# Expert results added onto the residual rows by indirect DMA, in place of a closing gather stage

## The reference, cut to what matters

```python
def _L1_ffn_ref(x, Wg, bg, W1, b1, W2, b2):
    gate_scores = x @ Wg + bg
    _, idx = jax.lax.top_k(gate_scores, K)                     # K = 2 of E = 8
    mask = jax.nn.one_hot(idx, E, dtype=x.dtype).sum(axis=-2)
    h = jax.nn.gelu(jnp.einsum('td,edh->teh', xf, W1) + b1[None], approximate=False)
    y = jnp.einsum('teh,ehd->ted', h, W2) + b2[None]
    out = jnp.einsum('ted,te->td', y, mf)
...
x = x + _L1_ffn_ref(_layernorm(x, axis=-1)[None], ...)[0]      # the residual is added last
```

## Time and profile before

| | us |
|---|---|
| median of 3 runs | 7423.68 (7422.31 to 7426.34) |
| the profiled execution | 7418.85 |
| its span, first to last instruction | 7417.1 |
| routing, about | 5878 to 6365 |
| filling, about | 6373 to 6390 |
| experts, about | 6390 to 7157 |
| closing, about | 7159 to 7417 |

### The profile page before, as it was taken

One profiled execution on the slowest core, in us unless ns is written; L12 is line 12 of the kernel. 1 busy time (PEld: TensorE's weight loads), 2 busy tenths in 40 slices (PEclk: granted clock), 3 DMA queues, 4 the chain that ended last, 5 costly groups with the idle time before them and its releaser, 6 DMA issues. The chain is left out here.

```text
span 7417.1 us, 130762 instructions
## 1 busy us (share of the span) xinstructions
PE 5086.8 (69%) x27158; PEld 4303.4 (58%) x27158; DVE 4225.4 (57%) x12806; ACT 2168.8 (29%) x5921; POOL 4011.9 (54%) x4739
## 2 busy tenths in 40 slices
PE   9955555555555699965267776777777666699950
PEld 3445555555555699963156555665665544699950
DVE  5565555555555433345567777777777677433333
ACT  3300000000000133322134444444444444466640
POOL 1157777777777400002377777777777377300027
PEclk9977777777777799988667777667767655799985
DMA  8843333333333211106544444444444333222246
GB/s 275 301 152 105 105 105 105 105 104 104 105 105 105 86 52 53 53 31 195 176 114 115 113 114 113 115 113 114 113 115 113 113 112 111 80 70 71 70 121 198
DMA packets 520513, 856.27 MB, mean 115 GB/s; under 512 B 99091, under 2 KB 378979, under 8 KB 519430
## 3 DMA queue, kind: packets, MB, share of 16 engines
q0 software_dynamic: 179568, 497.45, 24.1%
q1 hardware_dynamic: 210614, 228.31, 9.9%
q10 hardware_dynamic: 130144, 128.87, 5.0%
HBM read 615.20 MB, written 239.07 MB: 115 GB/s over the span
## 5 line engine op out<-in xcount | busy, mean ns | idle before, releaser
L1069 POOL DMA_INDIRECT s_rows<-xp_table,s_index x1664 | 1638.3, 985 | 506.9 <-issue 452.4
L323 POOL DMA_INDIRECT s_rows<-rel_table,s_staged x1664 | 1579.7, 949 | 535.3 <-issue 491.0
L352 PE MATMUL s_part<-s_pick,s_rows 128*128 128x128 f32 x6656 | 1196.5, 353 | 920.0 <-DMA s_rows<-rel_table,s_staged 688.8
L352 PEld LDWEIGHTS s_part<-s_pick,s_rows 128*128 128x128 f32 x6656 | 1106.9, 259 | 1010.0 <-DVE s_pick L360 959.0
L1190 PE MATMUL s_part<-s_pick,s_scaled 128*128 128x128 f32 x6656 | 1430.4, 374 | 371.3 <-DVE s_scaled L1346 354.0
L1190 PEld LDWEIGHTS s_part<-s_pick,s_scaled 128*128 128x128 f32 x6656 | 1206.5, 266 | 564.6 <-issue 289.0
L373 DVE TENSOR_TENSOR sums<-sums,s_part 128x256 f32 x1666 | 701.8, 421 | 931.5 <-PE s_part L352 747.6
L1361 DVE SCALAR_TENSOR_TENSOR sums<-sums,s_old_share,s_part 128x256 f32 x1666 | 793.1, 476 | 403.4 <-PE s_part L1190 253.3
L1103 ACT ACTIVATE s_apart<-window,s_local 128x128 f32<-128x128 f32 x1664 | 531.7, 390 | 1153.9 <-PE s_part L1190 1101.4
L1346 DVE TENSOR_TENSOR s_scaled<-s_rows,s_share 128x256 f32<-128x256 f32 x1664 | 687.1, 413 | 84.1 <-issue 83.0
L2126 POOL DMA_INDIRECT s_got<-y_rows,s_staged x196 | 189.0, 964 | 832.9 <-ACT s_staged L2100 774.5
(11 more groups left out here) (306 smaller groups left out, 6450.2 us busy)
## 6 DMA issues: line engine op xcount, KB each, us to landing
rel_table<-s_rows ACTq DMA_DIRECT2D x98, 1024.0 KB
s_rows<-rel_table,s_staged POOLq DMA_INDIRECT x1664, 2.7
s_rows<-xp_table,s_index POOLq DMA_INDIRECT x1664
s_rows<-exp_rows SPq DMA_DIRECT2D x204, 128.0 KB, 2.0
y_rows<-s_y SPq DMA_DIRECT2D x204, 128.0 KB, 1.7
s_x<-in_x SPq DMA_DIRECT2D x196, 128.0 KB, 2.2
s_mid<-mid_rows SPq DMA_DIRECT2D x98, 256.0 KB
x_rows<-s_x SPq DMA_DIRECT2D x196, 128.0 KB, 1.7
```

Source lines behind the costliest of these rows:

```text
L323: pool.indirect_dma_start(out=rows[:, s, :], out_offset=None, in_=rel_table[:, :], in_offset=bass.IndirectOffsetOnAxis(ap=staged[:, 2 * s ...
L352: mm = pe.matmul(part[s % PARTS][:, k, :], rows[:, s, k * P:(k + 1) * P], pick[:, s % PICKS, :], start=True, stop=True)
L1069: pool.indirect_dma_start(out=rows[:, b * BATCH + s, :], out_offset=None, in_=xp_table[:, :], in_offset=bass.IndirectOffsetOnAxis(ap=index ...
```

## The change

`x3_rows` becomes `sums_out`, which the routing stage fills with the residual rows as before. The rows of `exp_rows` grow from 256 to EXT = 264 floats, and ACT writes each row's token number into element 256 (one more ACT operation per tile); the filling rows carry numbers from NP on, which name spare rows behind the tokens. In the expert stage POOL turns the token numbers of each loaded tile into integers (`keep_ids`), waits for `y` and for the DMA of the tile before, and issues one indirect DMA that adds `y` onto `sums_out` (`add_to_out`). SP no longer stores `y`, and its next load waits for `keep_ids` too. DVE's buffer of `y` is free again when the adding DMA of two tiles before has landed. When all 204 have landed, SP and ACT each copy one half of `sums_out` to `out` by a plain DMA. The closing stage, `y_rows`, `place_all`, `mask_all` and the six operations that used them go.

```diff
-    x3_rows = dram("x3_rows", [NP, D])
-    exp_rows = dram("exp_rows", [X * CAP + X * P, D])
-    y_rows = dram("y_rows", [TILES * P, D])
+    sums_out = dram("sums_out", [NP + P, D])
+    exp_rows = dram("exp_rows", [X * CAP + X * P, EXT])
...
-                        pool.wait_ge(moved_done, 2 * t + 2)
+                        pool.wait_ge(moved_done, 3 * t + 3)
                         pool.sem_inc(scatter_go, 1)
...
+                    pool.iota(token_i[:, :], pattern=[[P, NT]], base=0, channel_multiplier=1).then_inc(const_i, 1)
+                    pool.wait_ge(const, 4)
...
-                        act.activation(moved[:, b, :].rearrange("p (k c) -> p k c", k=HALVES), sums[:, :, ds(t * P, P)], ACT.Copy).then_inc(moved_done, 1)
+                        act.activation(moved[:, b, 0:D].rearrange("p (k c) -> p k c", k=HALVES), sums[:, :, ds(t * P, P)], ACT.Copy).then_inc(moved_done, 1)
+                        act.activation(moved[:, b, D:D + 1], token[:, ds(t, 1)], ACT.Copy).then_inc(moved_done, 1)
...
-                        v.tensor_scalar(mask_all[:, ds(t, 1), :].rearrange("p o x -> p (o x)"), rank[:, b, :], 2.0, None, ALU.is_lt)
...
-                        v.tensor_copy(place_all[:, ds(t, 1), :].rearrange("p o x -> p (o x)"), place[:, b, :]).then_inc(place_step, 1)
...
+                    v.tensor_scalar(zeros[:, D:D + 1], line[:, :], float(NP), None, ALU.add).then_inc(zero_made, 1)
...
-                    then(v.tensor_tensor(place_all[:, :, :], place_all[:, :, :], shift[:, :].unsqueeze(1).broadcast_to([P, NT, X]), ALU.add))
-                    then(v.tensor_tensor(place_all[:, :, :], place_all[:, :, :], mask_all[:, :, :], ALU.mult))
-                    then(v.tensor_reduce(both[:, :], place_all[:, :, :], AX.X, ALU.add))
-                    then(v.tensor_reduce(second[:, :], place_all[:, :, :], AX.X, ALU.max))
-                    then(v.tensor_tensor(slots[:, :, 0], both[:, :], second[:, :], ALU.subtract))
-                    then(v.tensor_copy(slots[:, :, 1], second[:, :]))
...
+            def copy_out(eng, k):
+
+                eng.wait_ge(y_out, 16 * TILES)
+                half = slice(k * (NP // 2), (k + 1) * (NP // 2))
+                eng.dma_start(out[half, :].rearrange("(q r) d -> q (r d)", r=16),
+                              sums_out[half, :].rearrange("(q r) d -> q (r d)", r=16)).then_inc(copied, 16)
+                eng.wait_ge(copied, 32)
...
-                    def store(t, b):
-                        sp.wait_ge(y_done, t + 1)
-                        sp.dma_start(y_rows[ds(t * P, P), :], y[:, b, :]).then_inc(y_out[b], 16)
-
                     def step(t, i, b, left):
                         if left == 2:
                             sp.wait_ge(turned, t + 1)
+                            sp.wait_ge(ids_kept, t + 1)
                             load(t + 2, b)
-                        if not isinstance(t, int) or t > 0:
-                            store(t - 1, 1 - b)
 
                     load(0, 0)
                     load(1, 1)
                     by_tiles(sp, step, TILES // 2)
-                    store(TILES - 1, (TILES - 1) % 2)
-                    for b in range(2):
-                        sp.wait_ge(y_out[b], 16 * (TILES // 2))
+                    copy_out(sp, 0)
+
+                @block.gpsimd
+                def _(pool):
+                    def keep_ids(t, i, b, s):
+                        pool.wait_ge(rows_in[b], 16 * i + 16)
+                        pool.sem_inc(ids_go, 1)
+                        pool.tensor_copy(ids[:, s, :], rows[:, b, D:D + 1]).then_inc(ids_kept, 1)
+
+                    def add_to_out(t, b, s):
+
+                        pool.wait_ge(y_done, t + 1)
+                        wait_past(pool, y_out, 16 * t)
+                        pool.wait_ge(ids_kept, t + 1)
+                        pool.sem_inc(out_go, 1)
+                        pool.indirect_dma_start(out=sums_out[:, :], in_=y[:, b, :], in_offset=None,
+                                                out_offset=bass.IndirectOffsetOnAxis(ap=ids[:, s, :], axis=0),
+                                                compute_op=ALU.add).then_inc(y_out, 16)
+
+                    for t in range(2):
+                        keep_ids(t, 0, t, t)
+                    for t in range(2):
+                        keep_ids(t + 2, 1, t, t + 2)
+                        add_to_out(t, t, t)
+                    with pool.Fori(0, TILES // 4 - 1) as i:
+                        for j in range(4):
+                            keep_ids(4 * i + j + 4, 2 * i + 2 + j // 2, j % 2, j)
+                            add_to_out(4 * i + j + 2, j % 2, (j + 2) % 4)
+                    for t in range(TILES - 2, TILES):
+                        add_to_out(t, t % 2, t % 4)
+                    pool.wait_ge(y_out, 16 * TILES)
...
-                        wait_past(v, y_out[b], 16 * i)
+                        wait_past(v, y_out, 16 * t - 16)
                         v.tensor_tensor(y[:, b, :], psY[b], b2_now[:, b, :], ALU.add).then_inc(y_done, 1)
...
-        with ExitStack() as st:
-            x3 = at(st, "s12_x3", [P, RING, D])
...
```

More of the change, by code:

```diff
@@ L50 @@
 TILES = 2 * NT + X
-RING = 7
+IDS = 4
 EXT = D + 2 * HEADS
@@ L1517, in gnn_kernel @@
             staged = at(st, "s9_staged", [P, 2, 2], I32)
-            moved = at(st, "s9_moved", [P, 2, D])
+            moved = at(st, "s9_moved", [P, 2, EXT])
+            token_i = at(st, "s9_token_i", [P, NT], I32)
+            token = at(st, "s9_token", [P, NT])
             psX = [bank(st, f"s9_psX{b}", D) for b in range(2)]
@@ L1542, in step @@
                         sp.wait_ge(x3_done, t + 1)
-                        sp.dma_start(x3_rows[ds(t * P, P), :], x3[:, b, :]).then_inc(x3_out[b], 16)
+                        sp.dma_start(sums_out[ds(t * P, P), :], x3[:, b, :]).then_inc(x3_out[b], 16)
                     load(0, 0)
@@ L1635, in move @@
                         act.activation(staged[:, b, :], slots[:, ds(t, 1), :].rearrange("p o j -> p (o j)"), ACT.Copy).then_inc(moved_done, 1)
-                        act.activation(moved[:, b, :].rearrange("p (k c) -> p k c", k=HALVES), sums[:, :, ds(t * P, P)], ACT.Copy).then_inc(moved_done, 1)
+                        act.activation(moved[:, b, 0:D].rearrange("p (k c) -> p k c", k=HALVES), sums[:, :, ds(t * P, P)], ACT.Copy).then_inc(moved_done, 1)
+                        act.activation(moved[:, b, D:D + 1], token[:, ds(t, 1)], ACT.Copy).then_inc(moved_done, 1)
                     hold(0, 0)
                     hold(1, 1)
+                    act.wait_ge(const, 4)
+                    for b in range(2):
+                        act.activation(moved[:, b, D + 1:EXT], window[:, 0:EXT - D - 1], ACT.Copy)
                     exp_below(0, 0)
@@ L1811, in last_places @@
                         note(t, b)
-                    v.wait_ge(const_i, 3)
+                    v.wait_ge(const_i, 4)
+                    v.tensor_copy(token[:, :], token_i[:, :]).then_inc(const, 1)
                     v.tensor_scalar(lower[:, :, :], lower_i[:, :, :], 0.5, None, ALU.is_gt).then_inc(const, 1)
@@ L1845, in gnn_kernel @@
             shift = at(st, "s10_shift", [P, X])
-            both = at(st, "s10_both", [P, NT])
-            second = at(st, "s10_second", [P, NT])
             over = at(st, "s10_over", [1, TILES, X])
@@ L1904, in _ @@
                     then(v.tensor_scalar(tile_exp[:, :], exp_f[:, :], float(X - 1), None, ALU.min))
[L1906 to L1911 removed]
         scores_of.close()
         with ExitStack() as st:
[L1917 removed]
+            rows = at(st, "s11_rows", [P, 2, EXT])
+            ids = at(st, "s11_ids", [P, IDS, 1], I32)
             hT = at(st, "s11_hT", [P, 2, HALVES, P])
@@ L1926, in gnn_kernel @@
             psY = [bank(st, f"s11_psY{b}", D) for b in range(2)]
-            rows_in, y_out = [sem(f"s11_rows_in{b}") for b in range(2)], [sem(f"s11_y_out{b}") for b in range(2)]
+            rows_in, y_out = [sem(f"s11_rows_in{b}") for b in range(2)], sem("s11_y_out")
+            ids_go, ids_kept, out_go = sem("s11_ids_go"), sem("s11_ids_kept"), sem("s11_out_go")
+            copied = sem("s11_copied")
             w1_go, w1_ready, w2_go, w2_ready, b2_ready = (sem(f"s11_{n}") for n in ("w1_go", "w1_ready", "w2_go", "w2_ready", "b2_ready"))
             turned, hT_ready, up_done, active, down_done, y_done = (sem(f"s11_{n}") for n in ("turned", "hT_ready", "up_done", "active", "down_done", "y_done"))
+            def copy_out(eng, k):
[4 more added lines that the diff above has]
+                eng.wait_ge(copied, 32)
             def expert(eng, t):
@@ L1992, in _ @@
                     by_tiles(act, step, TILES // 2)
+                    copy_out(act, 1)
                 @block.tensor
```

92 lines of the change are left out of this document (12 added, 80 removed).

## The result

| | before | after |
|---|---|---|
| median of 20 runs each, us | 7423.52 (7418.7 to 7429.5) | 7439.92 (7434.34 to 7448.0) |
| the profiled execution | 7418.85 | 7448.0 |
| its span | 7417.1 | 7446.3 |
| first y of the expert stage starts | 6401.2 | 6414.7 |
| last y starts | 7157.0 | 7395.0 |

The ratio after to before is 1.0022, with a 95% interval of 1.0015 to 1.0028: the change makes the kernel slower by 16 us, 0.2%. 7231 was forecast, in a range of 7180 to 7400; the result lies outside both. Rival (3), the chain of adding DMAs that takes over the expert stage, had named 7455.

The account below looks back on a forecast made before the run. TensorE was taken to bound the expert stage, POOL the routing and closing stages. Last y's end 7157.4 + 5.1 + 66 + 1.9, less 5 and 0.5, gave a span of 7225, a median of 7231 us; range 7180 to 7400.

Parts of the forecast that it names:

- Rival (3): Expert stage: the chain of adding DMAs takes over and eats the whole gain; 4.8 us a tile, 7455 us, slower; chance 0.12.
- The adding DMAs: Expert stage: landing taken as 3.0 us, between 2.4 and 4.4; chain 3.4 us a tile, hidden by TensorE's 3.72.
- The cover: Expert stage: the room in which TensorE's 3.72 us a tile hides the chain, up to a landing of 3.3 us.
- The reissue: Expert stage: 0.40 us from POOL's instruction before to the adding DMA's issue, added to the landing for each tile.
- The tail: End of the expert stage: the last adding DMA lands 5.1 us after the last y.
- The copy: After the last add: plain copy from memory to memory, 66 us with issue and landing; bounds 32 and 125.
- Routing: Routing stage, bounded by POOL: two DVE operations go, taken as -5 us, ends -20 and +5.
- Filling: Filling stage: DVE's six last operations go and POOL takes DVE's place, -0.5 us.
- The closing stage: After the last y: the stage is removed, and all 259.7 us to the span's end go.
- (1): Expert stage: adding DMA lands after 3.3 to 4.2 us; 7329, or 7370 with a lower TensorE clock; chance 0.22.
- (2): Expert stage: DVE's copies stretch POOL's issue; 7237 with 0.35 us, 7370 with the whole 0.99; chance 0.13.
- (4): Final copy: carried by few DMA engines, it takes 250 us instead of 64; 7417 us; chance 0.03.

## Why the prediction was wrong

**The adding DMAs: here it failed.** "I take 3.0" for the landing; it is 4.0, inside the stated ends of 2.4 and 4.4 and near the upper. The cover ended at 3.3. I had added to a scatter the 0.3 by which a gather is dearer and 0.3 for the second stream at the bulk rate. Neither prices what the runs showed, an add that costs 1.6 us over the plain scatter and grows with the rows (2.9, 3.4 and 4.0 for 32, 64 and 128). The upper end had been built from what the DMA does, a whole read and then a whole write, and would have been the better choice, 0.4 us off where 3.0 was 1.0 off.

**The reissue, in the same sum: failed too.** 0.4 us came from rows in which POOL followed an instruction of its own with no wait. Behind a wait it is 0.83. The two misses add up to 1.00 + 0.43, over a cover of 0.32 (3.72 less the 3.4 of the sum): 1.11 us a tile, 226 us by 204 tiles, against 224.5 measured. At a landing of 4.0 with my 0.4 the chain would have been 4.4 us, +139. With the true restart the cover ended at a landing of 2.89, below my own 3.0.

**The tail** was 8.6 us and not 5.1, by the same two terms. **The copy** was 41.9 us instead of 66, inside the bounds of 32 and 125: 12.85 MB in 41.9 us are 307 GB/s, and each byte is read and written. The Trainium skill (DMA: Bandwidth & Descriptors, Latency and other measured facts) has 207 to 214 GB/s per direction for copies with pieces of 16 KB and a harmless pitch. That is too low for this copy of pieces of 57 KB on two queues; the measurement decides. **Routing** gained nothing where 5 were taken: the scatter's mean fell from 1124 to 1095 ns, and POOL's busy time of the stretch stayed. **Filling** +1.8 instead of -0.5. **The closing stage** went as predicted, all 259.7 us. Two slips of the prediction's own arithmetic changed nothing: with the copy at 125 and routing at +5 its upper end is 7300 and not 7295, and "faster" adds up to 0.85 and a little more, not 0.84.

By terms, from the forecast span of 7225 to 7446.3: +224.5 stage, +3.5 tail, -24 copy, -1.5 end, +5 routing, +2.3 filling, +11.8 ahead of it all, together +221.6, the 221.3 between the spans but for rounding.

**The rivals.** (3) was right in its mechanism and its 4.8 us a tile, partly by luck: 4.4 + 0.4 where 4.0 + 0.83 stand. It had 0.12. (1) was right that the landing is above the cover, but its 3.3 to 4.2 were summed with the short restart, and its loss of the clock did not come: 1.00 at a PE busy for 82%. (2) is real and worth 0.2 us a tile, and only once the chain is on the path. (4) fell: the copy took 41.9 us, at a DMA share of 1.03 [the stretch 7410 to 7440 above].

Why (3) had so small a chance: the sum took 3.0, in the lower half of bounds 2.0 us apart, while the cover ended only 0.3 us above the value taken, and the 0.4 us of restart was not given bounds at all.

## What to carry to other kernels

A DMA that waits for the one before it costs landing plus restart per step, and the restart behind a wait has to be read from rows with a wait, not from a queue that runs freely. Before a chain is put beside a full engine, its period is compared with that engine's at the upper bound of each term; where it is not below, a second transfer in flight is the cheap insurance (here 0 instead of 1.11 us a tile). And where a DMA can add, it can add onto the output: leaving out the copy at the end gave 36 us.

## What the runs showed of the hardware

An indirect DMA of 128 rows of 1 KB that adds in memory is issued in 1.54 us at least (1.65 in the median), against 0.95 (0.98) for the same one without adding, and lands after 4.0 us against 2.4. Two of them in flight did not slow TensorE at a DMA share of 0.45. From the end of a y that GpSimd had waited for to the start of its next indirect DMA passed 0.92 us in the run without adding and 0.83 with two adds in flight; where a DMA released it, 0.83 us are left of the 4.83 of a tile after a landing of 4.0. TensorE kept its granted clock of 1.00 over 930 us with a gap of 0.8 to 0.9 us in most tiles.
